# Layer 0's routing placed behind the third batch of features, and its first scatters tied to later batches

## The reference, cut to what matters

```python
x = L0_attn_x                                  # (8, 512, 128)
xn = _layernorm(x)
x = x + _L0_attn_ref(xn, ...) + _L0_ffn_ref(xn, ...)
xn = _layernorm(x)
x = x + _L1_attn_ref(xn, ...) + _L1_ffn_ref(xn, ...)
```

```python
logits = jnp.einsum('bsd,ed->bse', x, router_w) + router_b     # 8 experts
weights, top1 = jnp.max(softmax(logits)), jnp.argmax(softmax(logits))
out = (x @ expert_w[top1].T + expert_b[top1]) * weights
```

## Time and profile before

| | |
|---|---|
| median of 3 runs | 823.16 us (821.97 to 823.99) |
| the profiled execution's own time | 828.99 us |
| its span, first to last instruction | 826.9 us |
| mean granted TensorE clock | 0.904 |
| busy: PE, DVE, ACT, POOL | 654.0, 448.2, 375.0, 245.3 us |

### The profile page before, as it was taken

The page is one execution under the profiler, slowest core; times in us unless marked ns, Lnnn a source line. Parts: engine busy times, 40 slices in busy tenths (PEclk is TensorE's granted clock), DMA queues, the critical chain, the costliest instruction groups (busy, mean ns, idle before and its releaser), DMA issues.

```text
span 826.9 us, 15605 instructions
## 1 busy us (share of the span) xinstructions
PE 654.0 (79%) x4213; PEld 542.3 (66%) x4217; DVE 448.2 (54%) x1243; ACT 375.0 (45%) x874; POOL 245.3 (30%) x292
## 2 busy tenths in 40 slices
PE   3859457763174799999999999999978899998950
PEld 3837346763073677777777787878757788887850
DVE  7488637751667867676776776676731111111116
ACT  2217414441023364646555555555314555555534
POOL 6065716656002222222222220000001343433430
PEclk9999669995555999999999999999967999999985
DMA  9992133341230000000000000000004444444539
GB/s 242 256 186 56 45 103 116 110 125 49 76 128 0 21 20 21 19 22 17 20 21 21 18 20 1 1 1 1 1 4 146 164 158 154 164 154 152 168 104 276
DMA packets 80840, 69.46 MB, mean 84 GB/s; under 512 B 8436, under 2 KB 66419, under 8 KB 80782
## 3 DMA queue, kind: packets, MB, share of 16 engines
q1 hardware_dynamic: 71616, 54.97, 23.9%
q0 software_dynamic: 6624, 12.70, 4.8%
q10 hardware_dynamic: 2542, 1.08, 0.5%
HBM read 22.63 MB, written 23.22 MB: 55 GB/s over the span
## 4 chain that ended last, share of the span: by engine, by line
PE 40%; issue 19%; SPq 19%; DVE 11%; DMA 6%; POOL 3%; ACT 1%; DVEq 1%; POOLq 0%; ACTq 0%; another core or an unknown queue 0%
PE psum L1424 9%; PE psum L1386 5%; PE psum L1405 5%; SPq L1097 5%; PE psum L1395 4%; SPq L1110 4%; PE psum L1432 3%; SPq L1120 3%; SPq L242 3%; DMA ydram<-arena,g_id 3%; PE psum L1371 3%; POOL ydram L819 2%; DMA arena<-ydram 2%; PE psum L1359 2%; PE psum L1380 2%
## 5 line engine op out<-in xcount | busy, mean ns | idle before, releaser
L678 POOL DMA_INDIRECT sorted<-xr_all,slot x96 | 94.7, 987 | 190.2 <-DVE arena L1654 162.7
L1209 POOL DMA_INDIRECT ydram<-arena,f_id x71 | 68.7, 967 | 241.4 <-DVE f_id L1185 220.5
L1550 ACT ACTIVATE arena<-arena 128x512 f32<-128x512 f32 x96 | 60.5, 630 | 133.9 <-DVE arena L1654 133.8
L1170 ACT ACTIVATE arena<-psum,b1T 128x128 f32<-128x128 f32 x284 | 81.2, 369 | 78.8 <-PE psum L1139 68.8
L1651 DVE TENSOR_REDUCE arena<-psum 128x8 f32<-128x512 f32 x96 | 66.4, 691 | 66.8 <-PE psum L1386 34.8
L1193 DVE TENSOR_TENSOR arena<-psum,b_bc 128x128 f32<-128x128 f32 x71 | 20.7, 292 | 145.5 <-PE psum L1150 74.8
L1424 PE MATMUL psum<-arena 128*128 128x66 f32 (+1 forms) x768 | 97.6, 267 | 0.1
L1424 PEld LDWEIGHTS psum<-arena 128*128 128x128 f32 x768 | 95.7, 196 | 0.3 <-ACTq L1556 0.3
L1139 PE MATMUL psum<-arena 128*128 128x128 f32 x568 | 82.4, 290 | 16.3 <-DMA arena<-arena 12.7
L1139 PEld LDWEIGHTS psum<-arena 128*128 128x128 f32 x568 | 71.3, 197 | 28.6 <-issue 21.6
L1150 PE MATMUL psum<-w,arena 128*128 x568 | 80.6, 285 | 0.4
(11 more groups left out here) (267 smaller groups left out, 1086.9 us busy)
## 6 DMA issues: line engine op xcount, KB each, us to landing
arena<-arena SPq DMA_DIRECT2D x71, 256.0 KB
arena<-ydram SPq DMA_DIRECT2D x24, 256.0 KB, 4.0
arena<-mix SPq DMA_DIRECT2D x40, 128.0 KB
sorted<-pre_row SPq DMA_DIRECT2D x1, 4680.0 KB
arena<-sorted SPq DMA_DIRECT2D x71, 65.0 KB
sorted<-pre_row SPq DMA_DIRECT2D x1, 2600.0 KB, 21.6
arena<-sorted SPq DMA_DIRECT2D x10, 260.0 KB, 3.1
x_all<-in_L_attn_x_dram SPq DMA_DIRECT2D x8, 256.0 KB, 5.4
```

What stands on the lines that cost most here:

```text
L678: g.indirect_dma_start(out=dst, out_offset=bass.IndirectOffsetOnAxis(ap=slot[:, choice, t:t + 1], axis=0), in_=xr_all[:, t, :], in_offset= ...
L1170: ins = act.activation(f_hT[rr % 4][:, j * P:(j + 1) * P], psum[:, 2 + rr % 2, j * P:(j + 1) * P], ACT.Relu, bias=b1T[:, bass.ds(e * FC + ...
L1209: g.indirect_dma_start(out=ydram, out_offset=bass.IndirectOffsetOnAxis(ap=f_id[rr][:, :], axis=0), in_=f_y[rr], in_offset=None, bounds_che ...
L1550: act.activation(c_p[s % 3], c_sx[s % 2], ACT.Exp).then_inc(c_pr, 1)
```

## The change

`two_deep` gets an optional third argument, a function that it calls once, before its second pair of stages, so behind the stage that brings batch 2. DVE, ACT and PE no longer run layer 0's routing ahead of the features but hand it to `two_deep` for that place. On POOL the first 16 scatters wait for later counts of `a_zqr`: scatters 0 to 3 for the queries of batch 3, and four more for each batch after it. On PE the norm matmuls of batch 2, which write PSUM bank 6, get a wait until routing's counts have been read. Layer 1 is unchanged.

```diff
-        def two_deep(eng, stage):
+        def two_deep(eng, stage, middle=None):
 
             stage(eng, None, (0, 0))
             for i in range(B // 2 - 1):
+                if middle and i == 1:
+                    middle(eng, 0)
                 stage(eng, (0, i), (1, i))
                 stage(eng, (1, i), (2, i))
...
                 elif t < 2 * B:
-                    g.wait_ge(a_zqr, 2 + t // 2)
+                    g.wait_ge(a_zqr, 2 + B // 2 + t // 4)
...
                 pe.wait_ge(a_nsu, b + 1)
+                if b == 2:
+                    pe.wait_ge(s_rt, 3)
...
             norm_act(act, 0)
-            routing_act(act, 0)
-            two_deep(act, feat_act)
+            two_deep(act, feat_act, routing_act)
...
             norm_dve(v, 0)
-            routing_dve(v, 0)
-            two_deep(v, feat_dve)
+            two_deep(v, feat_dve, routing_dve)
...
-            routing_pe(pe, 0)
             pe.wait_ge(s_bp, N_BP)
             pe.wait_ge(s_lgu, 1)
-            two_deep(pe, feat_pe)
+            two_deep(pe, feat_pe, routing_pe)
```

## The result

The kernel after took 844.27 us (median of 4 runs, 842.72 to 844.82), the kernel before 822.57 us beside it (4 runs, 820.5 to 823.99). The ratio is 1.0263, 95% interval 1.0236 to 1.029: 21.7 us slower, 19.4 to 23.9 by the interval. The forecast was 842.1 us, 18.9 slower. One execution of a kernel further down, `routing_alone`, took 2190.31 us; without it the median of that kernel is 856.55 us, and its ratio rests on the other five alone.

The account below looks back on a forecast made before the run. POOL's row of scatters was taken to set when the states start. Routing, first scatter and 31 free steps put the last start at 124.7 instead of 105.78: 823.16 + 18.9 = 842.1 us, range 838 to 846 (0.78).

Parts of the forecast that it names:

- What binds: SP's load of group 0, behind layer 0's last POOL scatter, starts the states; features end with 8.6 us to spare.
- Rival D: The last scatter doesn't gate the states; the features' 13.2 us count, less 8.6 of room: +4.6, 827.8 us; chance 0.03.
- The features start no earlier: PE's feature matmuls still wait for POOL's biases until about 51.5 us; POOL beside idle DVE gains 0.3 us.
- Rival B: POOL's bias chain runs much faster with DVE idle, features start early: 839.7 or 838.5 us; below 838, chance 0.05.
- The routing: On DVE, coming in at 68.75 us before batch 3, priced by layer 1's rows: 13.27 us, upper bound 17.07.
- rival A: DVE's routing stays at 17.07 us (+3.8, 845.9 us), and scatters meet line 876 (848.0); above 846, chance 0.12.
- The first scatter: On POOL, released 0.77 us after batch 3's line 876 is done at 83.11, so it starts at 83.88 us.
- 31 free steps: POOL's scatters at 1.278 us, 39.6 us, plus 1.2 of stretches; last start 124.7 instead of 105.78, 18.9 us later.
- Meetings of line 880 and scatters: Scatters beside DVE's line 876 (numbering before) cost nothing, 842.1 us; by the skill's port rule 2.1 us, 844.2.
- After the load: From group 0's load on, SP, PE and POOL keep order and data; the 18.9 us carry to the end unchanged.
- Rival C: The states take the delay up, group periods falling from 8.86 to below 6.76 us: 822 to 824 us; chance 0.02.
- These waits never hold anything: POOL's next waits, four scatters per batch: four take 5.1 us, a batch of features 4.06, so no cost.

Follow-up runs that it names:

- routing_alone: The kernel after with the scatters' waits of the kernel before (two scatters per batch): 856.55 us, ratio 1.0356.
- after_short_biases: The kernel after with POOL's preparation of the projections' biases cut to one copy, two of three bf16 parts left out: ratio 1.0264.
- front_no_waits: The kernel before, routing still in front, with the scatters' waits on the features taken out: 848.46 us, 2.6% slower.

## Why the prediction came out right, step by step

1. **What binds.** SP's load of group 0 behind the last scatter. Right in both kernels: line 773 was released by it with 16.58 us of idle PE ahead (14 forecast), and in the kernel before 10 us more on the features cost nothing. Rival D, by which 10 us there would show, is out for the kernel before. For the kernel after its own trace alone speaks: no experiment tests it there.
2. **The features start no earlier.** -0.3 us was taken from line 407; it went from 1.42 to 1.14 and the three of line 416 from 4.86 to 4.65. The lines between gave some more, so that POOL's last one ends 11.98 us behind line 397, before 12.72; but PE's first row of features comes only 0.36 us earlier, 12.82 us behind line 397, before 13.18. Rival B is out.
3. **The routing.** 13.27 us forecast (and called the lower bound), 13.16 measured, where the earlier trace rows had 17.07. The rows of layer 1 were the right price, and rival A's first half is out. ACT waited 3.96 us for DVE there, at line 870, and PE's norms of batch 2 came at 73.95, when the counts had been read; both were covered, as forecast.
4. **The first scatter** comes 0.99 us behind the end of line 880 (0.77 taken).
5. **31 free steps.** 40.82 us forecast, 41.19 measured. The two stretches, 0.43 and 0.98 us, lie at the roots and the first state, not at line 880.
6. **Meetings of line 880 and scatters.** No scatter got longer there; DVE's instruction did, twice in four meetings, by 0.28 and 0.26 us, and that was not on the path. By the estimate that the prediction drew from "SBUF — State Buffer", section "SBUF: two separate sides", in the Trainium skill, the scatters would have been held by 2.1 us. The trace has none of it at line 880. Beside DVE's longer tensor_scalar of line 900 (103.56 to 104.52) the scatter at 103.24 did take 1.40 us; whether that is the page's mechanism was not tested.
7. **After the load** the same lengths: 103.91 us to the first addition of `ydram` rows before and 104.25 after. Rival C is out.

The sum was 18.9. In the trace the load of group 0 came 19.48 us later, counted from line 397. The medians say 21.7, with 19.4 at the lower end of the interval. What the remaining 2 us are can't be told: the two profiled executions differ by more than that in stretches that the change doesn't touch. The one of the kernel after is shorter by 2.6 us in the setup and by 2.3 in layer 1's experts (176.16 against 178.44 us from DVE's first copy of the ids to its last addition), so that the two traces as wholes are only 14.0 us apart. The sum is borne out by the medians and by the stretch from line 397 to the load, not by that difference.

**What the prediction did not see.** "These waits never hold anything" is true of when the scatters start, and the second half of the change was priced by nothing else. But the earlier trace rows show the old waits doing two things: they delayed scatters, and they kept them apart. Every other kernel here that let scatters run back to back beside dense features for more than some 7 us got PE's signals late, from 1.2 us in the kernel before to 34. The kernel after did not, in its profiled execution, and its four times of 842.72 to 844.82 leave no room for it. Had it gone as the other two with the routing in the middle, the whole biases and nothing held did (ratios 1.0356 and 1.0399), the result would have been 852 to 855 us, outside of the range. No rival had this mechanism, and that the kernel after escaped it is luck as far as the prediction goes.

**What stays open.** Why PE's signals come late. What the runs exclude: the depth of POOL's queue (four in flight changes nothing), the place of the routing (the front and the middle both show it), and PE's placing alone (the kernel after and that with the hold at its end ran alike until then). What the others agree on: scatters at one per 1.28 us, for about 7 us or more, while PE works densely; where the row runs to its end, the last late rise comes 3.7 to 5.7 us after the last scatter has started. Why the kernel after escapes was not settled. Its trace differs in one more thing: it alone holds all 512 rises of the scatters' landings, 16 for each; the others hold 76 to 220 of them, the kernel before 220. So it isn't excluded that the recording takes part in the lateness or in the loss; every execution here has its granted clock on record, and none was taken without.

## What to carry to other kernels

A wait that holds a queue back may be keeping two engines apart. Before it is loosened, look at what runs beside the queue, and look in the new trace at when semaphores rise, not only at when instructions end. Price a moved step by the rows of the same code elsewhere in the trace (layer 1 here), not by its old place, where it shared the time with another engine. And try a close neighbour of a design too: a kernel with 10 us of work added under 16 us of idle time was 17 us slower.

## What was not expected of the hardware

- PE's semaphore rises came up to 34 us after the matmul's end (after_short_biases, keys of batch 7: 82.88 against 116.64; routing_alone: 94.2 against 126.77), while those recorded for DVE and ACT came within 0.13 us. In front_no_waits PE then also ran single matmuls that wait for nothing 1.4 to 3.5 us apart; in the batches before, two of them and the bias in front took 0.55.
- In routing_alone this happened with 32 scatters at 1.27 to 1.28 us each and about 53 GB/s in the stretch, at a share of 0.16 of the DMA engines, so not for want of bandwidth.
- A DVE instruction on 128x512 beside a scatter took 0.71 us in place of 0.43, and the scatter kept its 0.97. Two of the four that met a scatter kept their 0.43.
